# A DLRM tower on one core: the top-layer weights loaded and rounded earlier, and the last half's packs and last store spread over queues

## What is computed

```python
e = stack([tbl_f[ids[:, f]] for f in range(27)], axis=1)         # 2048 x 27 x 128
inter = einsum('bfd,bgd->bfg', e, e)                             # lower triangle: 351 pairs
z = concat([bottom, inter[:, TRIL]], axis=1)
h = concat([z, bottom], axis=1)                                  # 128 + 351 + 128 = 607 columns
h = relu(h @ W_top1 + b_top1)                                    # 512
h = relu(h @ W_top2 + b_top2)                                    # 256
y = h @ W_top3                                                   # 1
```

## Time and profile before

| what | value |
|---|---|
| median of 3 executions | 378.96 us (377.74 to 380.42) |
| the profiled execution's own time | 379.7 us |
| its span | 377.9 us |
| TensorE matmul busy | 341.6 us, 90% |
| GpSimd busy | 263.0 us, 70% |
| VectorE busy | 248.2 us, 66% |
| ScalarE busy | 145.9 us, 39% |
| mean granted TensorE clock | 0.982 |

### The profile page before, as it was taken

One profiled execution on the slowest core, in us unless ns is written; L12 is line 12 of the kernel. 1 busy time (PEld: TensorE's weight loads), 2 busy tenths in 40 slices (PEclk: granted clock), 3 DMA queues, 4 the chain that ended last, 5 costly groups with the idle time before them and its releaser, 6 DMA issues.

```text
span 377.9 us, 10285 instructions
## 1 busy us (share of the span) xinstructions
PE 341.6 (90%) x4321; PEld 330.9 (88%) x4321; DVE 248.2 (66%) x332; ACT 145.9 (39%) x280; POOL 263.0 (70%) x283
## 2 busy tenths in 40 slices
PE   0667857979899999999999999999999999999996
PEld 0566657979899999999999999999999999998985
DVE  3689994868459918794669546982879456962051
ACT  1467762262531354134431553135313443146202
POOL 6777777777777777777777777777777777773030
PEclk9979998998999999999999999999999999999999
DMA  7987749233724264435333352435343533322230
GB/s 172 232 200 216 193 113 305 68 90 76 241 79 117 68 193 108 107 80 188 111 89 84 94 201 72 105 74 191 104 104 81 187 112 89 82 63 73 51 29 1
DMA packets 46905, 45.76 MB, mean 121 GB/s; under 512 B 32944, under 2 KB 35782, under 8 KB 46860
## 3 DMA queue, kind: packets, MB, share of 16 engines
q1 hardware_dynamic: 35950, 27.04, 26.9%
q0 software_dynamic: 8896, 17.89, 17.0%
q10 hardware_dynamic: 2014, 0.18, 0.4%
HBM read 39.52 MB, written 5.55 MB: 119 GB/s over the span
## 4 chain that ended last, share of the span: by engine, by line
PE 82%; DVE 6%; DMA 4%; ACT 3%; issue 3%; SPq 1%
PE work L441 41%; PE gram L468 14%; PE work L453 6%; PE work L494 4%; PE work L495 4%; PE work L496 4%; DMA raw_lo<-in_tbl 4%; DVE onehot L601 3%; PE work L511 2%; PE work L513 2%; PE work L512 2%; PE work L522 2%; DVE tab_lo L586 2%; SPq L331 1%; DVE w_lo L611 1%
## 5 line engine op out<-in xcount | busy, mean ns | idle before, releaser
L411 POOL DMA_INDIRECT emb<-in_tbl,ids_all x272 | 259.1, 953 | 84.0 <-issue 80.2
L601 DVE TENSOR_TENSOR onehot<-ids_bc,row_idf 125x1024 fp32r<-125x1024 int32 (+2 forms) x232 | 199.0, 919 | 38.2 <-PE work L441 32.6
L441 PE MATMUL work<-onehot,tab_hi 125*128 125x256 f32 x672 | 172.7, 296 | 24.9 <-ACT tab_hi L707 13.0
L441 PE MATMUL work<-onehot,tab_lo 125*128 125x256 f32 x672 | 168.9, 290 | 2.5 <-issue 2.5
L441 PEld LDWEIGHTS work<-onehot,tab_hi 125*128 125x128 f32 x672 | 133.5, 199 | 33.5 <-issue 18.5
L441 PEld LDWEIGHTS work<-onehot,tab_lo 125*128 125x128 f32 x672 | 133.9, 199 | 0.0
L749 ACT COPY embT<-work 128x512 f32<-128x512 f32 (+1 forms) x36 | 26.8, 797 | 103.3 <-PE work L441 103.3
L468 PE MATMUL gram<-embT 128*54 128x52 f32 x1920 | 51.5, 214 | 2.4 <-ACT embT L571 2.2
L468 PEld LDWEIGHTS gram<-embT 128*54 128x54 f32 x1920 | 49.5, 130 | 4.7 <-issue 1.4
L756 ACT COPY inter<-gram 118x416 f32<-118x416 f32 x64 | 32.4, 507 | 16.7 <-PE gram L468 15.8
L494 PE MATMUL work<-x_hi,w_hi 128*128 128x256 f32 (+1 forms) x128 | 36.9, 288 | 1.8 <-DVE embT L571 0.9
(11 more groups left out here) (55 smaller groups left out, 220.5 us busy)
## 6 DMA issues: line engine op xcount, KB each, us to landing
ids_bc<-in_sel_ids SPq DMA_DIRECT2D x14, 512.0 KB, 4.4
grams<-inter SPq DMA_DIRECT2D x64, 84.5 KB
emb<-in_tbl,ids_all POOLq DMA_INDIRECT x272
ids_bc<-in_sel_ids SPq DMA_DIRECT2D x11, 256.0 KB, 8.6
misc<-in_tbl SPq DMA_DIRECT2D x3, 448.0 KB
inter<-in_tbl SPq DMA_DIRECT2D x3, 448.0 KB
misc<-in_bottom SPq DMA_DIRECT2D x8, 128.0 KB
raw_w<-in_W_top SPq DMA_DIRECT2D x4, 256.0 KB, 7.4
```

The lines of the kernel that those rows point to most:

```text
L411: pool.indirect_dma_start(out=emb[:, t % TILE_SLOTS, f, :], out_offset=None, in_=gather_tables[f], in_offset=bass.IndirectOffsetOnAxis(ap= ...
L441: mm = nc.tensor.matmul(out, part[0:k, CHUNK_AT[f] + c, :], onehot[0:k, at % RING, i * HALF:(i + 1) * HALF], start=(c == 0 and i % 2 == 0 ...
L601: nc.vector.tensor_tensor(onehot[0:k, at % RING, 0:width], ids_bc[0:k, four[0]:four[-1] + 1, :].rearrange("p i n -> p (i n)"), row_idf[0:k ...
```

## The change

- SP issues the first-layer weights behind the last three staged tables (chunk `CH`, the two bottom blocks, behind table 7; chunk 2 with the bias behind table 8; chunk 1 behind table 9), and chunk 0 and the second layer's weights behind the first one-hot ids of half 1.
- VectorE adds the two bottom blocks before one-hot 5 of half 1 instead of one-hot 13. ScalarE rounds all weights right after `extract_all(0)`, before `select_out(1, 0)`. The rests stay before one-hot 13.
- In the last half each pack is loaded in two DMAs, one for each tile: those of tile 14 as soon as it is stored and the packed buffer is free (SP 7 before the last store and 6 after its part of it, ScalarE 6, GpSimd 9), those of tile 15 after its store (SP 12, ScalarE 12, GpSimd 4).
- The last tile's store is issued by SP (two DMAs) and ScalarE (two).

```diff
+    EARLY_POOL = PACKS[2::3]
+    EARLY_FIRST, EARLY_SECOND, EARLY_ACT = [[pack for pack in PACKS if pack not in EARLY_POOL][n::3] for n in range(3)]
...
+        def load_packs_of_tile(eng, t, packs, loaded):
+            at = t % 2 * QUADS
+            for f, g, n, c, k in packs:
+                eng.dma_start(packed[k:k + n, c, at * QS:(at + QUADS) * QS].rearrange("k (s n) -> k s n", s=QUADS),
+                              grams[t, :, f, g:g + n, :].rearrange("s k n -> k s n")).then_inc(loaded[c], 16)
...
+                if n >= NSEL - 3:
+                    load_w1(X_ORDER[n - (NSEL - 3)])
...
             def store(t):
                 sp.wait_ge(extracted, (t + 1) * GRAMS)
-                for q in range(QUADS):
-                    ...
+                store_quads(sp, t, range(QUADS if t + 1 < TILES else TWO))
+                if t + 1 == TILES:
+                    load_packs_of_tile(sp, t - 1, EARLY_SECOND, packs_loaded)
                 sp.wait_ge(stored, 16 * QUADS * (t + 1))
...
                 load_ids(1, j)
+                if j == 0:
+                    load_w1(X_ORDER[CH])
+                    sp.dma_start(raw_w2[:, 1, :, :], w_top2.rearrange("(c p) n -> p c n", p=P)).then_inc(w2_loaded, 16)
...
             sp.dma_start(bot[:, :, :], bottom_v[0]).then_inc(bot_loaded, 16)
-            load_weights()
...
+                if h + 1 == HALVES:
+                    sp.wait_ge(packed_split, CH * h)
+                    load_packs_of_tile(sp, 2 * h, EARLY_FIRST, packs_loaded)
                 store(2 * h + 1)
...
-                load_packs(sp, h, PACKS if h + 1 < HALVES else SP_PACKS, packs_loaded)
+                if h + 1 < HALVES:
+                    load_packs(sp, h, PACKS, packs_loaded)
+                else:
+                    load_packs_of_tile(sp, 2 * h + 1, SP_PACKS, packs_loaded)
...
             pool.wait_ge(packed_split, CH * (HALVES - 1))
+            pool.wait_ge(stored, 16 * QUADS * (TILES - 1))
+            load_packs_of_tile(pool, TILES - 2, EARLY_POOL, packs_pool)
             pool.wait_ge(stored, 16 * QUADS * TILES)
-            load_packs(pool, HALVES - 1, POOL_PACKS, packs_pool)
+            load_packs_of_tile(pool, TILES - 1, POOL_PACKS, packs_pool)
...
             for n in range(len(ONEHOTS[1])):
+                if n == RING:
+                    sum_w1_bottom()
...
             extract_all(0)
+            for c in X_ORDER:
+                round_w1(c)
+            round_w2()
             select_out(1, 0)
             extract_all(1)
             rows_all(2)
-            for c in X_ORDER:
-                round_w1(c)
-            round_w2()
...
             last = HALVES - 1
+            act.wait_ge(extracted, TILES * GRAMS)
+            store_quads(act, TILES - 1, range(TWO, QUADS))
             act.wait_ge(packed_split, CH * last)
+            load_packs_of_tile(act, TILES - 2, EARLY_ACT, packs_loaded)
             act.wait_ge(stored, 16 * QUADS * TILES)
-            load_packs(act, HALVES - 1, ACT_PACKS, packs_loaded)
+            load_packs_of_tile(act, TILES - 1, ACT_PACKS, packs_loaded)
```

More of the change, by code:

```diff
@@ L65, in dlrm_tower @@
     SP_PACKS, ACT_PACKS = [[pack for pack in PACKS if pack not in POOL_PACKS][n::2] for n in range(2)]
-    POOL_PACKS_OF = [len([pack for pack in POOL_PACKS if pack[3] == c]) for c in range(CH)]
+    EARLY_POOL = PACKS[2::3]
+    EARLY_FIRST, EARLY_SECOND, EARLY_ACT = [[pack for pack in PACKS if pack not in EARLY_POOL][n::3] for n in range(3)]
+    POOL_PACKS_OF, EARLY_POOL_OF = [[len([pack for pack in packs if pack[3] == c]) for c in range(CH)] for packs in (POOL_PACKS, EARLY_POOL)]
     assert CH == 3
@@ L307, in by_tile, with store_quads @@
             return bank(*key)[:, 0:HALF].rearrange("d (s t b) -> d t s b", s=QUADS, t=2)
+        def load_packs_of_tile(eng, t, packs, loaded):
[3 more added lines that the diff above has]
+                              grams[t, :, f, g:g + n, :].rearrange("s k n -> k s n")).then_inc(loaded[c], 16)
+        def store_quads(eng, t, quads):
+            for q in quads:
+                row, col = q // TWO * SIDE + q % TWO * NF, q % TWO * NG
+                eng.dma_start(grams[t, q, 1:NF, :, :], inter[row + 1:row + NF, col:col + NG, :]).then_inc(stored, 16)
         def load_packs(eng, h, packs, loaded):
@@ L318, in _, with load_w1 @@
         def _(sp):
+            def load_w1(c):
+                if c == CH:
+                    sp.dma_start(raw_w1[:, 1, CH, :], w_top1[0:D, :]).then_inc(w1_loaded[CH], 16)
+                    sp.dma_start(raw_w1[:, 0, CH, :], w_top1[D + PAIRS:, :]).then_inc(w1_loaded[CH], 16)
+                else:
+                    sp.dma_start(raw_w1[0:PAIR_ROWS[c], 1, c, :], w_top1[D + c * P:D + c * P + PAIR_ROWS[c], :]).then_inc(w1_loaded[c], 16)
+                if c == CH - 1:
+                    sp.dma_start(raw_w1[ONES:ONES + 1, 1, c, :], b_top1.rearrange("(o n) -> o n", o=1)).then_inc(w1_loaded[c], 16)
             sp.dma_start(ids_all[:, 0:2, :], ids_v[:, 0:2, :]).then_inc(ids_loaded[0], 16)
@@ L339, in load_ids @@
                 sp.dma_start(ids_bc[:, some, :], sel_ids[h][:, some, :].to_broadcast([P, len(four), HALF])).then_inc(ids_bc_loaded[j], 16)
-            def load_weights():
-                for c in X_ORDER:
[L344 to L351, removed]
             def store(t):
                 sp.wait_ge(extracted, (t + 1) * GRAMS)
-                for q in range(QUADS):
-                    row, col = q // TWO * SIDE + q % TWO * NF, q % TWO * NG
-                    sp.dma_start(grams[t, q, 1:NF, :, :], inter[row + 1:row + NF, col:col + NG, :]).then_inc(stored, 16)
+                store_quads(sp, t, range(QUADS if t + 1 < TILES else TWO))
+                if t + 1 == TILES:
+                    load_packs_of_tile(sp, t - 1, EARLY_SECOND, packs_loaded)
                 sp.wait_ge(stored, 16 * QUADS * (t + 1))
@@ L384, in _ @@
                     sp.dma_start(bot[:, :, :], bottom_v[2]).then_inc(bot_loaded, 16)
-                if h:
+                if 0 < h < HALVES - 1:
                     sp.wait_ge(packed_split, CH * h)
-                else:
-                    sp.wait_ge(ones_ready, 1)
-                load_packs(sp, h, PACKS if h + 1 < HALVES else SP_PACKS, packs_loaded)
+                elif h == 0:
+                    sp.wait_ge(ones_ready, 1)
+                if h + 1 < HALVES:
+                    load_packs(sp, h, PACKS, packs_loaded)
+                else:
+                    load_packs_of_tile(sp, 2 * h + 1, SP_PACKS, packs_loaded)
             is_freed(sp, "y", 0)
@@ L603, in one_hot, with sum_w1_bottom @@
                                         row_idf[0:k, ROW_AT[chunks] + c:ROW_AT[chunks] + c + 1].to_broadcast([k, width]), ALU.is_equal).then_inc(onehot_ready, 1)
+            def sum_w1_bottom():
+                dve.wait_ge(w1_loaded[CH], 32)
+                nc.vector.tensor_tensor(raw_w1[:, 1, CH, :], raw_w1[:, 1, CH, :], raw_w1[:, 0, CH, :], ALU.add).then_inc(w1_bot_summed, 1)
             def split_w1(c):
                 k = X_ROWS[c]
-                if c == CH:
-                    dve.wait_ge(w1_loaded[c], 32)
-                    nc.vector.tensor_tensor(raw_w1[:, 1, c, :], raw_w1[:, 1, c, :], raw_w1[:, 0, c, :], ALU.add).then_inc(w1_bot_summed, 1)
                 dve.wait_ge(w1_hi_ready, X_ORDER.index(c) + 1)
@@ L643, in round_last @@
                 is_filled(dve, "mlp2", h - 1, M2 - 1)
-                dve.wait_ge(packs_loaded[c], 16 * (PACKS_OF[c] * (h + 1) - POOL_PACKS_OF[c]))
-                dve.wait_ge(packs_pool[c], 16 * POOL_PACKS_OF[c])
+                dve.wait_ge(packs_loaded[c], 16 * (PACKS_OF[c] * (h + 2) - POOL_PACKS_OF[c] - EARLY_POOL_OF[c]))
+                dve.wait_ge(packs_pool[c], 16 * (POOL_PACKS_OF[c] + EARLY_POOL_OF[c]))
                 nc.vector.tensor_copy(x_hi[0:k, PAIRS_AT + c, :], packed[0:k, c, :]).then_inc(packed_hi_ready, 1)
```

## The result

| what | before | after |
|---|---|---|
| median, 22 executions of each | 379.05 us | 377.87 us (376.72 to 379.31) |
| ratio | | 0.9963, 95% interval 0.9950 to 0.9976 |
| the profiled execution's own time | 379.7 us | 377.31 us |
| its span | 377.9 us | 375.5 us |

The change gains 0.4% by the ratio, 1.2 us by the medians. The forecast was 376.7 us, 0.6%; for the profiled execution 377.2 us, where it has 377.31.

A forecast was written before the change was run, and what follows sets the result against it. TensorE looked like the bound, with GpSimd's gathers close behind. Of 8.2 us saved early (4.2 + 4.05) 2.5 arrive: 379.7 - 2.5 = 377.2 us profiled, 376.5 against the median, 376.7 with unpriced crossings; range 374.4 to 380.3.

The forecast's parts named there:

- Weights loaded early: Half 1's first select: TensorE's 2.54 us pause and the 1.65 us of slow clock behind it go, 4.2 us.
- rounded early: Before half 1's one-hot 13: VectorE's wait for ScalarE's rounding goes, and TensorE's pause and slow clock with it, 4.05 us.
- The gathers take over from tile 9 on: From tile 9 TensorE waits for gathered rows at each odd tile's last transpose group, about 1.5 us a half.
- Of 8.2 us, 2.5 arrive.: At tile 15's last transpose group TensorE goes on at 345.85 instead of 348.35 us, so only 2.5 us are gained.
- The room: TensorE's slack behind the gathered rows at an odd tile's last transpose group: 2.5 us at tile 15, 8.4 at tile 7.
- The prediction's own sign of being wrong: Among the signs: tile 15's products not following the last gather's start by 3.9 us.
- The clock at the end: At tile 15, pauses of 1.5 and 1.14 us: no clock fall, cost 0; rival, a fall costing 1.7 us, chance 0.22.
- With 4.05 it is the same 2.5.: If the first pause stays, the front's lead is 4.05 us, and 2.5 us still arrive at tile 15.
- The last half, 0: After tile 15's transposes: packs that land earlier and the store over two queues are worth 0.
- The pause near 60 us: Half 1's first select: TensorE's 2.54 us pause is its instructions arriving late behind DMA data, and goes.

The follow-up runs named there:

- Without the gathers' limit: The last gathered table's gather left out from tile 2 on (14 of 272): 0.9797, median 371.53 us on the changed kernel; 0.9983, 378.32 us on the kernel before.
- the copies: Changed kernel, with SP also copying the two weight matrices (1.8 MB) from DRAM to DRAM where it loaded the weights before: 0.9981 of the kernel before.
- one chunk of 1.45 us: Changed kernel with the first chunk of mlp1 of half 6 (12 matmuls) ahead of tile 15's last transpose group: 0.9918 of the kernel before, median 375.45 us.
- bolder moves: Changed kernel, two mlp1 chunks ahead in half 7; in halves 4 to 6 mlp1 whole, or one chunk, ahead of the odd tile's last group: 0.9933, 0.9946 of before.
- the front with the moved chunk and the old tail: Changed kernel with store and last-half packs as before, first mlp1 chunk of half 6 ahead of tile 15's last group: 0.9962 of the kernel before.
- the old rounding with the moved chunk: Changed kernel with weights summed and rounded at the old place, first mlp1 chunk of half 6 ahead of tile 15's last group: 0.9926 of the kernel before.

## Why the prediction was right, and where it was off

The number lies in the range, the direction is right, and the profile has the predicted shape. Of the 2.3 us that were forecast below the median on record, the medians show 1.2. Step by step:

- *Weights loaded early, 4.2 us; rounded early, 4.05 us.* Right together for the profiled executions: tile 2's products start 7.7 us earlier, and half 2's first select at 103.31 us. Without the gathers' limit 6.8 us arrive in the medians and 9.0 in the spans (378.2 to 369.2). Of the 9.0, 1.6 us are spread between executions, there already when tile 0's products begin (57.74 against 56.15), ahead of both pauses. And of the 8.2, 3.4 us are low clock, which the profiled execution had and many others have not: over 70 executions of the kernel before, taken beside these experiments, the 22 with a mean granted clock up to 0.984 (the profile has 0.982) have a median of 379.8 us, the 33 with 0.994 or more one of 378.4. At 0.994 TensorE can't have lost over 2.3 us to the clock in all. So the median execution had less to gain than the profiled one.
- *The gathers take over from tile 9 on, about 1.5 us a half.* Right, with waits of 1.04 to 1.25 us.
- *"Of 8.2 us, 2.5 arrive."* The room was worked out with 2.3 us from the last gather's start to the use of its rows, and this term was too small. Four profiles show it directly: 3.03 (342.87 to 345.90), 2.95 (343.53 to 346.48), 3.03 (343.96 to 346.99) and 3.11 us (343.53 to 346.64). For a gather that runs alone, 2.3 was nearly right: in the kernel before, the last gather of a group lands 2.4 to 2.5 us after its start where neither a store nor an instruction block moves beside it (ten cases, by the trace's landing events). But the lead itself takes that away. Tile 14's pairs are now stored at 342.77 us instead of 346.44, beside the last gather, since TensorE brings them earlier. SP's store in the changed kernel, then all queues from 1.5 to 3.3 us after the gather's start, in the changed kernel and in the kernel before:

```profile
342.77 1.56 SPq L323 DMA_DIRECT2D grams<-inter  x4
...
q1 hardware_dynamic: 91, 0.18, 28.1%
q0 software_dynamic: 32, 0.07, 14.8%
...
q0 software_dynamic: 32, 0.07, 13.8%
q8 instruction: 1, 0.02, 3.4%
```

  q1 carries the store. In each of the nine profiles in which it moves beside the last gather, the gather lands 2.9 to 3.1 us after its start. That the store is the cause wasn't tested by itself. In the kernel before, that gather was late too, by another thing: 15 of its 16 parts land by 2.52 us, the last at 3.69 (347.2 us), behind the instruction block. So the room in that one execution was 1.1 us, and 2.3 undisturbed.

  That the profiled pair still differs by 2.4 us is luck: this execution's last gather began 0.67 us sooner (342.87), and the rows were there at 345.90, where 345.85 was forecast. Over the profiles of these experiments with all gathers it began between 342.61 and 344.00. The prediction's own sign of being wrong, products that don't follow the last gather's start by 3.9 us, came: they follow it by 4.73.
- *The clock at the end.* I took no fall as the likelier. The changed kernel's profile has none, at pauses of 1.25 and 1.05 us; with 1.40 and 1.05, and with 1.65 and 1.04, it fell. The 22 executions of the changed kernel make two bunches, 14 from 376.72 to 377.95 and 8 from 378.41 to 379.31. The fall, 1.4 us, may be what parts them. The mean granted clock of each execution leans that way (median 0.9925 in the lower bunch, 0.986 in the upper), but the two overlap (0.984 to 1.000 and 0.937 to 0.993), and a mean doesn't say where the clock fell. So this is argued and not shown, and why the medians differ by only 1.2 us stays partly open.
- *"With 4.05 it is the same 2.5."* Wrong. Loading early alone gave 1.0004, and the copies, which bring the first pause back and leave the early rounding, 0.9981. The room was filled, but the size of the last pause, and by it the clock, does hang on how TensorE's lead falls out over the halves: there it was one wait, of 1.65 or 1.40 us, instead of four.
- *The last half, 0.* Right (0.9994). GpSimd's nine early packs began at 346.9 us, earlier than the 350 to 352 of the prediction even with the 2.3 us that tile 15's products come sooner, and none was late.
- *The pause near 60 us.* Right. That it is made by DMA traffic is shown by the copied bytes, and that it is the instructions that come late by the times of the instruction blocks, as far as q8 is TensorE's. The Trainium skill (Runtime: NRT & Kernel Launch, Instruction fetch mechanics) has fetching mostly hidden; behind tile 0's products, at a DMA share of 1.06 and 1.21, it was not.

## What to carry to other kernels

An engine at 100% need not be the bound: compare the pace of every engine that waits for nobody, here 42.6 against 41.1 us a half, and work out how much room the faster one still has at the last meeting point. What a change upstream can bring ends there. Then put work into the wait that it uncovers, just enough for it: one chunk of 1.45 us in a wait of 1.25 brought as much again as the whole change, and bolder moves brought no more. It did so only with the packs spread, which by themselves were worth nothing. And look at what the lead moves along with it: here a store that now runs beside the gather everyone waits for.

## What was not expected of the hardware

- A short wait is worth more than its length when the granted clock falls behind it. 1.65 us and 1.04 us of pause, 0.66 us of work between them, were followed by a clock of 0.59 over 4 us and 1.4 us of loss; 1.25 and 1.05 us were not. A single wait of 2.04 us was followed by 0.50, while single waits of 1.86 us (tile 3 of the front with the moved chunk and the old tail) and 1.64 us (tile 13 of the old rounding with the moved chunk) left the clock at 1.00.
- A gather of 128 rows of 512 bytes takes 3.0 us from its start on GpSimd to the matmul that waits for it where a store moves beside it, and lands after 2.4 to 2.5 us where nothing does.
- 1.8 MB of copies that nobody waits for stopped TensorE for 2.23 us, by a 16 KB block of instructions that moved some 2.5 us late.
